# Adapter input products from each sample's own gathered columns, and a new order of VectorE's last additions

## What is computed

```python
def _lora_linear(x, W, A, B, adapter_indices):
    base = jnp.einsum('bsd,df->bsf', x, W)
    Ai = A[adapter_indices]
    Bi = B[adapter_indices]
    lora = jnp.einsum('bsr,brf->bsf', jnp.einsum('bsd,bdr->bsr', x, Ai), Bi)
    return base + lora
gate = _lora_linear(x, Wg, Ag, Bg, adapter_indices)
up = _lora_linear(x, Wu, Au, Bu, adapter_indices)
h = jax.nn.silu(gate) * up
return _lora_linear(h, Wd, Ad, Bd, adapter_indices)
```

## Time and profile before

| | |
|---|---|
| median of 3 runs | 1266.41 us (1262.3 to 1268.48) |
| the profiled execution | 1263.87 us, span 1261.8 us |
| PE busy | 1249.3 us, 99% of the span |
| DVE busy | 977.8 us, 77% |
| POOL busy | 665.7 us, 53% |
| ACT busy | 559.2 us, 44% |

### The profile page before, as it was taken

How to read it: one execution, slowest core, us unless ns; L and a number is a source line. 1 busy time by engine, 2 the same in 40 slices (tenths; PEclk the granted TensorE clock), 3 DMA queues, 4 the chain that set the end, 5 groups by cost and what they waited for, 6 DMA issues and landing times.

```text
span 1261.8 us, 17908 instructions
## 1 busy us (share of the span) xinstructions
PE 1249.3 (99%) x6204; PEld 1041.9 (83%) x6204; DVE 977.8 (77%) x1554; ACT 559.2 (44%) x993; POOL 665.7 (53%) x549
## 2 busy tenths in 40 slices
PE   8999999999999999999999999999999999999998
PEld 7788888888888888888888888888888888888886
DVE  6987777886788777788779768777888877777775
ACT  3744445444344444454444444444443434444432
POOL 4476555555635556545554556565555444445453
PEclk9999999999999999999999999999999999999999
DMA  5856345555965345445687444535477732243333
GB/s 193 299 177 221 121 119 166 159 146 170 378 203 189 105 122 150 128 131 175 218 316 218 158 126 147 153 120 136 146 289 267 229 93 89 70 117 101 118 92 109
DMA packets 141097, 210.11 MB, mean 167 GB/s; under 512 B 43473, under 2 KB 87761, under 8 KB 141009
## 3 DMA queue, kind: packets, MB, share of 16 engines
q1 hardware_dynamic: 118128, 137.03, 34.7%
q0 software_dynamic: 22016, 70.80, 17.0%
q10 hardware_dynamic: 864, 1.15, 0.2%
HBM read 164.89 MB, written 44.04 MB: 166 GB/s over the span
## 4 chain that ended last, share of the span: by engine, by line
PE 90%; DVE 5%; DMA 2%; issue 1%; ACT 1%; another core or an unknown queue 0%; SPq 0%; DVEq 0%; ACTq 0%
PE px L1544 28%; PE pd L1544 27%; PE py L1544 14%; PE pz L1544 7%; PE pz L1561 3%; PE pv L1590 2%; PE pv L1588 2%; PE pd L1822 2%; PE py L1561 2%; PE px L1561 1%; DVE wg_lo L1215 1%; DMA w_raw<-w_gu 1%; PE pd L1571 1%; PE pd L1665 0%; PE pd L1793 0%
## 5 line engine op out<-in xcount | busy, mean ns | idle before, releaser
L687 POOL TENSOR_TENSOR h_lo<-g,h_hi 128x512 fp32r<-128x512 f32 x127 | 184.3, 1451 | 336.2 <-ACT h_hi L809 335.5
L656 POOL DMA_INDIRECT b_got<-b_table,idx_b x192 | 197.5, 1029 | 58.5 <-issue 49.0
L1544 PE MATMUL px<-xo_hi,wg_hi 128*128 128x512 f32 x540 | 216.9, 402 | 2.1 <-ACT up L809 0.7
L1347 DVE TENSOR_TENSOR acc<-pd,acc 128x512 f32<-128x512 f32 x252 | 168.0, 686 | 63.0 <-PE pd L1544 59.9
L1215 DVE TENSOR_TENSOR wg_lo<-w_raw,wg_hi 128x512 fp32r<-128x512 f32 (+1 forms) x268 | 192.1, 720 | 31.1 <-issue 19.5
L1544 PE MATMUL px<-xo_hi,wg_lo 128*128 128x512 f32 x540 | 211.8, 392 | 0.0
L1544 PE MATMUL px<-xo_lo,wg_hi 128*128 128x512 f32 x540 | 210.4, 390 | 0.0
L809 ACT ACTIVATE wg_hi<-w_raw 128x512 fp32r<-128x512 f32 (+1 forms) x272 | 153.0, 570 | 114.9 <-PE py L1561 70.3
L1544 PE MATMUL pd<-wd_hi,h_hi 128*128 128x512 f32 x512 | 202.8, 396 | 0.0
L1544 PE MATMUL pd<-wd_lo,h_hi 128*128 128x512 f32 x512 | 201.0, 393 | 0.0
L1544 PE MATMUL pd<-wd_hi,h_lo 128*128 128x512 f32 x512 | 199.8, 390 | 0.0
(11 more groups left out here) (292 smaller groups left out, 2403.1 us busy)
## 6 DMA issues: line engine op xcount, KB each, us to landing
w_raw<-w_gu SPq DMA_DIRECT2D x68, 512.0 KB
wd_raw<-w_dn SPq DMA_DIRECT2D x64, 256.0 KB
xo_hi<-xops SPq DMA_DIRECT2D x21, 512.0 KB, 5.9
xo_lo<-xops SPq DMA_DIRECT2D x21, 512.0 KB, 6.9
acc<-x SPq DMA_DIRECT2D x8, 1024.0 KB, 8.4
ad_raw<-ad_table SPq DMA_DIRECT2D x16, 512.0 KB
xops<-st_hi SPq DMA_DIRECT2D x24, 256.0 KB, 2.7
xops<-st_lo SPq DMA_DIRECT2D x24, 256.0 KB, 2.9
```

The lines of the kernel that those rows point to most:

```text
L656: gp.indirect_dma_start(out=dst, out_offset=None, in_=rows_of, in_offset=bass.IndirectOffsetOnAxis(ap=rows.bitcast(U32), axis=0)).then_inc ...
L687: return gp.tensor_tensor(dst, src_raw, src_hi, ALU.subtract)
L1347: ins = dve.tensor_tensor(dst, pd[j][:, :], dst, ALU.add)
L1544: ins = pe.matmul(psum, w_parts[wi], x_parts[xi], start=(start and i == 0), stop=(stop and i == 2), skip_group_check=more)
```

## The change

**Own columns.** For quarters 1 to 3, 16 gathers (`gather_own`) fetch for each sample the A columns of its own adapter, gate and up, into `st_lo`: 128 rows of 512 bytes a gather. ACT and DVE split them into four groups of 128x512 in place of the adapters' weight groups; one extra subtraction (`own_difference`) makes the second half's weights. `own_products` replaces the 7 products: 24 matmuls of 256 columns for each half. There are now two results in place of four. `c11`, `u3`, `c12`, the `sums` of unit -1 and its weight load are gone, and two `ua_high` and two `ua_low` remain. `select` keeps its 12 matmuls, and for these quarters uses one fixed `sel_own`, so `selectors` is gone there. ACT makes `sel_own` once, with 12 small activations in block 14 of quarter 0, from 9 small DVE instructions in block 13.

**Moves.** POOL's 16 gathers stand in blocks 13 (5, after `h_low(q, 13, 1)`), 14 (2 before `h_low(q, 14, 1)`, 5 after it) and 15 (4, ahead of `h_low(q, 15, 0)`). The four `gather_ad` move from blocks 13 and 14 to behind block 15 and into unit -1, their stores on SP too. DVE's `v_low(q, 0)`, `own_difference` and two low parts stand between the additions of the last two down phases. SP loads A22 ahead of S2, and the weights of block 0 in block 14. Small index tiles share `f_one`.

**The end.** `finish(3, 0)` is cut up: pair 0, `v_mask(3, 1)`, pair 1, `v_low(3, 1)`, pairs 2 and 3.

The core of the diff:

```diff
+            def own_products(q, t):
+                for cp in range(2):
+                    k = ((A11, A12), (S1, A22))[t][cp]
+                    tokens_ready(q, k)
+                    pe.wait_ge(w_done[2 * t + cp], unit(q, -1) + 1)
+                    w_parts = own_homes(2 * t + cp)
+                    for c in range(2):
+                        for a in range(2):
...
+                            for i, (wi, xi) in enumerate(((0, 0), (0, 1), (1, 0))):
+                                ins = pe.matmul(ua_bank(q, t, 0)[:, a * HALF:(a + 1) * HALF], w_parts[wi][:, cols],
+                                                (xo_hi, xo_lo)[xi][:, k, tok], start=(cp == c == a == i == 0),
+                                                stop=True, skip_group_check=True)
+                ins.then_inc(own_mm, 1)
...
@@ PE, the units @@
-                adapters = b == -1
+                if b == -1:
+                    pe.wait_ge(c12_done, k)
+                    own_products(q, 0)
+                    pe.wait_ge(c21_kept, k)
+                    own_products(q, 1)
+                    pe.wait_ge(down_add, 5 * q * 2 * SUPER)
+                    finish(q - 1, 0)
+                    pe.wait_ge(c22_done, k)
+                    select(q, 0)
+                    continue
...
@@ POOL, the units @@
                 if b % 2:
-                    gp.wait_ge(c11_done, n)
+                    gp.wait_ge(c11_done, k)
                     ad_low(q, b // 2)
...
+                if to_own and b == BLOCKS - 1:
+                    gather_own(q + 1, range(12, 16))
                 gathers = b % 2 and (q, b) != (QUARTERS - 1, BLOCKS - 1)
                 if (q, b) != (0, 0):
                     h_low(q, b, 0)
...
-                if b == BLOCKS - 2 and q + 1 < QUARTERS:
-                    for g in range(2, AD_GROUPS):
-                        gather_ad(q + 1, g)
+                if to_own and b == BLOCKS - 2:
+                    gather_own(q + 1, range(5, 7))
...
                 if b == BLOCKS - 3 and q + 1 < QUARTERS:
-                    for g in range(2):
-                        gather_ad(q + 1, g)
+                    gather_own(q + 1, range(0, 5))
+                if to_own and b == BLOCKS - 2:
+                    gather_own(q + 1, range(7, 12))
+                if to_own and b == BLOCKS - 1:
+                    for g in range(4):
+                        gp.wait_ge(w_done[g], n + 2)
+                    for g in range(2):
+                        gather_ad(q + 1, g)
...
@@ ACT, the units @@
+                if b == -1:
                     v_lower(q - 1, 0)
                     v_high(q - 1, 0)
+                    weights_high(n, 3)
                     v_lower(q - 1, 1)
+                    ua_high(q, 0)
+                    weights_high(n + 1, 0)
+                    weights_high(n + 1, 1)
+                    weights_high(n + 1, 3)
+                    ua_high(q, 1)
+                    v_high(q - 1, 1)
+                    weights_high(n + 1, 2)
+                    continue
...
+                if (q, b) == (0, BLOCKS - 2):
+                    act.wait_ge(sel_mm, 2)
+                    act.wait_ge(slots_done, 1)
+                    for m in range(2):
+                        for s in range(HS + 2):
...
+                            ins = act.activation(sel_own[:, m, :, lo:hi], pattern_kept[:, :, 0:hi - lo], ACT.Copy,
+                                                 scale=slot_mask[:, at:at + 1])
+                    ins.then_inc(sel_done, 1)
...
@@ DVE, the units @@
                 if b == -1:
-                    v_low(q - 1, 0)
-                    c11(n)
-                    u3(n)
-                    ua_low(q, 0, 0)
-                    c12(n)
-                    ua_low(q, 1, 1)
-                    ua_low(q, 0, 1)
                     sums(n + 1)
+                    ua_low(q, 0)
                     weights_low(n + 1, 0)
-                    ua_low(q, 1, 0)
+                    weights_low(n + 1, 1)
+                    finish(q - 1, 0, (0,))
+                    ua_low(q, 1)
+                    finish(q - 1, 0, (1,))
                     select(q, 0)
-                    weights_low(n + 1, 1)
+                    finish(q - 1, 0, (2, 3))
                     weights_low(n + 1, 2)
-                    finish(q - 1, 0)
                     weights_low(n + 1, 3)
-                    selectors(q, 1)
                     continue
...
-                c11(n)
+                c11(k)
+                if to_own:
+                    weights_low(n + 1, 0)
...
                     if last and phase_at[2]:
-                        finish(q, 0)
+                        finish(q, 0, (0,))
+                        v_mask(q, 1)
+                        finish(q, 0, (1,))
                     if last:
                         v_low(q, phase_at[2])
+                    if last and phase_at[2]:
+                        finish(q, 0, (2, 3))
+                    if to_own and not phase_at[2]:
+                        v_low(q, 0)
+                        own_difference(q + 1)
+                        weights_low(n + 1, 2)
+                        weights_low(n + 1, 3)
```

More of the change, by code:

```diff
@@ L315, in cond_resid_kernel @@
         down_add = sem("down_add")
+        own_got = [sem(f"own_got{t}") for t in range(2)]
+        own_diff = sem("own_diff")
+        own_mm = sem("own_mm")
+        slots_done = sem("slots_done")
         ua_hi_done = sem("ua_hi_done")
@@ L741, in _ @@
                         gather_bd(q - 1, 1)
+                        for g in range(2, AD_GROUPS):
+                            gather_ad(q, g)
                     continue
@@ L941, in _ @@
                     ad_high(q, b // 2)
+                k = blocks_done(q, b)
+                to_own = b == BLOCKS - 1 and not last
                 if b == -1:
@@ L1041, in _ @@
                     keep_c21()
-                act.wait_ge(p3_mm, n)
-                if not last and b > 1:
+                act.wait_ge(p3_mm, k)
+                if not last and not to_own and b > 1:
                     weights_high(n + 1, 2)
@@ L1059, in _ @@
                     weights_high(n + 1, 2)
-                if not last:
+                if not last and not to_own:
                     weights_high(n + 1, 3)
@@ L1348, in add_down @@
                     ins.then_inc(down_add, 1)
-                if m == SUPER - 1:
+                if m == SUPER - 1 and not ends:
                     v_mask(q, t)
@@ L1370, in finish, with own_difference, ua_low @@
                     dve.tensor_tensor(dst, finish_bank(q, t, j)[:, :], dst, ALU.add).then_inc(y_add, 1)
-            def ua_low(q, t, m):
-                src = ((g0, up0), (g1, up1))[t][m] if q else first_banks[t][m]
-                dve.wait_ge(ua_hi_done, 4 * q + ua_order(q, t, m))
-                dve.tensor_tensor(h_lo[:, t, m, :], src[:, :], h_hi[:, t, m, :], ALU.subtract).then_inc(ua_done, 1)
+            def own_difference(q):
+                dve.wait_ge(own_got[1], q * 2 * TP * 16)
+                first, last_two = (own(cp)[:, 2 * TP:QS, :, :] for cp in range(2))
+                dve.tensor_tensor(last_two, last_two, first, ALU.subtract).then_inc(own_diff, 1)
+            def ua_low(q, t, m=0):
+                dve.wait_ge(ua_hi_done, ua_made(q, t, m))
+                dve.tensor_tensor(h_lo[:, t, m, :], ua_bank(q, t, m)[:, :], h_hi[:, t, m, :], ALU.subtract).then_inc(ua_done, 1)
             def c11(n):
@@ L1492, in _ @@
                     half_numbers()
-                if not last and not late:
+                if (q, b) == (0, BLOCKS - 3):
+                    dve.wait_ge(layer_mm, QP)
+                    dve.tensor_copy(pattern_kept, pattern)
+                    for at in range(2 * HS):
+                        ins = dve.tensor_scalar(slot_mask[:, at:at + 1], p_f[:, 0:1], float(at), None, ALU.is_equal)
+                    ins.then_inc(slots_done, 1)
+                if not last and not late and not to_own:
                     sums(n + 1)
@@ L1515, in _ @@
                     token_low(q, parts_at(q, b))
-                c12(n)
+                c12(k)
                 gate0()
```

328 lines of the change are left out of this document (179 added, 149 removed).

## The result

The changed kernel took 1268.48 us in the median of 20 runs (1266.11 to 1270.74), the kernel before beside it 1263.70 (1261.26 to 1268.48): ratio 1.0034, 95% interval 1.0027 to 1.0041. I had predicted 1261.6 with a range up to 1266.5, a gain of 4.8 us; it is a loss of 4.8. (The forecast stood on a median of 3 runs, 1266.41, which is 2.7 above the kernel before as measured here; on that base a gain of 4.8 would have been 1258.9.) No measurable difference at 0.5%, but the sign and the range are wrong. The experiments measured the same program four times more: 1.0043 on one chip, and 1.0003, 0.9999 and 0.9997 on two others. So there are two things to explain: why nothing is gained where I expected 4.8, and why the result and one of the chips lose 4 to 6 more.

The account below looks back on a forecast made before the run. PE, busy for 99% of the span, was taken as the bound. The sum -11.9 + 6.6 + 0.3 + 1.0 + 0.1 - 0.9 = -4.8 us gave a predicted median of 1261.6 us, range 1254.5 to 1266.5.

Parts of the forecast that it names:

- The mechanism of the gain: PE's products in unit -1: 9.61 us replaced by 5.64, saving 3.97 a unit, 11.9 in all.
- the products do not shrink: Rival on PE's own products: 256 columns cost more, for example 0.17 us each; +2.8, 1269.2 us; chance 0.04.
- That delay is not added to the other: Quarter boundary: A22's wait and h_low(15, 0)'s lateness share the same clock time, so only one is charged.
- the block of DVE by POOL: Block 15: POOL's subtractions hold DVE's low parts ahead of u3, so A22 waits up to 2.4 us.
- the lateness of `h_low(15, 0)`: Block 15: behind four gathers it ends at 333.3, PE needs it at 331.09; PE waits 2.2 us.
- the 6.6 of the sum: PE's wait of 2.2 us for POOL's h_low(15, 0) at three boundaries, with ends 0 and 9.0.
- The gathers' price: POOL's 16 gathers in blocks 13 to 15: 1.275 us each, making h_low(15, 0) end at 333.3.
- DVE at the boundary: After the last down phase (end T): ua_low(1) ends at T + 8.5, needed at T + 8.8; 0.3 us in all.
- shared reading adds up: Rival at the boundary: A22's wait also delays h(15, 0), 3.7 us a boundary; -0.3, 1266.1 us; chance 0.12.
- The selectors: Block 14 of quarter 0: ACT's twelve activations delay u3, so A22 waits 1.0 us once (ends 0 and 1.3).
- The end: Kernel end: PE's 0.96 us wait for v_low goes; gain 0.9 us (ends 0 and 1.0).
- Gathers landing late: Rival at the boundary: the last gathers land past 11 us, each boundary loses 3.7 us more; 1273 us; chance 0.06.

Follow-up runs that it names:

- e1: Changed kernel with DVE's two low parts of the own columns behind gate0 of block 15 instead of ahead of u3: 1259.07 us, 0.9974 of the kernel before.
- f3: e1 measured again, beside f0_after on the same chip: 1259.23 us, 0.9979 of the kernel before.
- e8: Changed kernel with POOL's gathers 9 to 11 moved behind the two down_low and ahead of ad_low, DVE's order kept: 1259.30 us, 0.9968 of the kernel before.
- g2: e8 with ACT's twelve selector activations split into two sixes: 1259.89 us, 0.9979 of the kernel before.
- after_again: The changed kernel measured again without an edit: 1263.11 us, 1.0003 of the kernel before.
- f0_after: The changed kernel without an edit, as control of other runs on the same chip: 1262.31 us, 0.9999 of the kernel before.
- e5: The kernel before with only the change's new order of DVE's last additions at the end: 1261.86 us, 0.9992 of the kernel before.
- e6: e1 with POOL's queue in block 15 reordered, two gathers ahead of each h_low: 1265.02 us, 1.0009 of the kernel before.
- e9: e6 with ACT's selectors in two sixes and POOL's four bd gathers issued ahead of three b_got gathers: 1274.07 us, 1.0087 of the kernel before.

## Why the prediction was wrong

**The mechanism of the gain held.** 48 matmuls at 0.1175 were to take 5.64 us; they took 5.78. Saved per unit: 3.83 for 3.97, in all 11.5 for 11.9. The rival "the products do not shrink" is out.

**The wait had the size I gave; its place was the other one of the two.** "That delay is not added to the other" held. I had both delays, priced the block of DVE by POOL at up to 2.4 and the lateness of `h_low(15, 0)` at 2.2, and said that PE pays for one of them only. I put the price on POOL's; the one that PE meets first is `u3`. It costs 2.0 to 2.1 us, 6.3 in all for the 6.6 of the sum, and masks the second, which is an idle time of 1.46 in e1 and costs 1.7 there. The gathers' price held too: in PE's time `h_low(15, 0)` ended at 332.7 (336.59 less 3.92), for 333.3.

**The first step that failed: the sum has no clock in it.** The granted clock was 1.00 wherever I read it, and I charged each wait in the middle of dense matmuls with its length alone. Yet 11 of the 27 waits for `u3` of 1.75 to 1.94 us in the traces are followed by a stretch at 0.50, and each such stretch cost 1.7 us. The changed kernel's mean clock on P and R is 0.9980 to 0.9982, the kernel before's 0.9995 to 0.9998: 0.0016 of 1262 us is 2.0, the largest single item of the error there. In the result's own runs the mean was 0.9973. The kernels that got rid of those waits (e1, f3, e8, g2) have 0.9994 to 0.9996.

**The second step that failed: "DVE at the boundary", "ua_low(1) ends at T + 8.5".** I charged 0.3 for it, with ends 0 and 3. On P it held: T + 8.15 in after_again. In the result's execution it was T + 11.0, since ACT could take t = 0 only at T + 7.25. PE stood 2.4 us ahead of the three blocks 0 in place of my 0.3, and 1.6 more ahead of `finish`, where the sum has nothing. These 4.0 us are most of what turns nothing into the loss of 4.8; on Q, with 5.8, it is the same. I had let the signal of t = 0 come when its matmuls are done, and nothing in the rows of before that I read says otherwise. Why it comes late stays open. It does so in the stretch in which PE dispatches a matmul every 0.12 us, new through this change, while the DMA engines are full (share 1.03). Both hold on P and R as well, where nothing stalls, so together they are not enough; that either has a part in it was argued, not shown.

**Of shared SBUF the trace's reading was right.** The Trainium skill ("SBUF — State Buffer", who interferes with whom), as I read it, would have let DVE in behind each single POOL instruction. The earlier trace rows had shown a subtraction held through two; here a low part was held through all that were left of the three (327.44 to 330.05), and e8 shows it unhindered. It was so at every boundary of the nine traces with this order: the low part ended 0.5 to 0.6 us behind the last of POOL's, whether it had begun in the first of them or in the second. None shows DVE get in between consecutive POOL subtractions. On P and R the rival "shared reading adds up" came nearest (a gain of 0.3), and in the result's runs "the products do not shrink" (a loss of 2.8), both by luck: `h_low(15, 0)` cost nothing on top of `u3`, and the products did shrink.

**The small terms.** The selectors cost 0.9 for 1.0. The end gave 0.84 for 0.9. DVE at the boundary cost nothing on P. Not in the sum were waits for bd, 0.3 to 1.1 an execution, and 0.2 to 0.5 more than before for ACT (up), together some 1 us. The sum with these sizes: -11.5 + 6.3 + 0.9 - 0.8 + 1.0 + 2.0 = -2.1, where the ratios say +0.4, -0.1 and -0.4 on P and R, each with an uncertainty of 1.1 to 1.5. So some 2 us are not accounted for. Matmul by matmul, from 60 us on, after_again gains 2.9 us on the trace of before and f0_after 1.5, about what the sum has for one clock drop and for two. What is missing would then lie ahead of that, where single executions differ by as much: the five traces of the changed kernel stand there from 0.4 us ahead of before's to 1.6 behind it, and e5's 1.4 ahead. Whether the change costs something there isn't shown.

**Gathers landing late** did not occur for the own columns; it did for bd once the other waits were gone (e6), by POOL's queue and the full engines together. My range ended at 1266.5, since I had let the terms left at zero add nothing: clock, bd and late signals can only add, and they did.

## What to carry to other kernels

When work is added ahead of a queue's subtractions, look not only at who waits for them, but at what stands on the other engine at the time to which they move: here a push of 4.6 us put them on top of two-input subtractions of DVE, and keeping them apart (e8) was worth as much as moving the victim (e1). Where two delays fall into the same stretch of time, charge the one that PE meets first, and know that the second comes up when the first is removed; then the third. A wait of 1.8 to 1.9 us between dense matmuls cost nearly twice its length (1.9 + 1.7) in 11 cases of 27 here, since the clock can fall behind it: give such a wait that price with a chance. And measure such a kernel beside its control on the same chip.

## What the runs showed of the hardware

- A DVE subtraction with both inputs in SBUF stood through three consecutive POOL subtractions (3.2 to 3.3 us for 0.7 of work; 2.6 where it began in the second of them) and ended 0.5 to 0.6 us behind the last of them, at every boundary of nine traces. With POOL's subtractions elsewhere it took its usual time (e8).
- Behind 11 of 27 waits of PE of 1.75 to 1.94 us, in an execution behind none to two of its three, came a stretch at 0.50 of the clock, which cost 1.7 us each time. Behind 13 waits of 1.45 to 1.53 it never came, nor behind the two of 1.81 (e8, g2) and the one of 2.27 (the result's execution); what decides it is not shown. On P a mean clock of 0.9979 to 0.9988 goes with the first kind, 0.9995 to 0.9996 with the second.
- 256 columns behind a full weight load cost 0.120 us in a stream of 48, for 0.1175 in a group of four.
- In such a stream, with the DMA engines full, ACT could take the result of t = 0 only at T + 6.7 to 7.3 in the result's execution and at T + 6.7 to 8.3 on Q (10.7 and more in e9), where PE's dispatch also stood still for 0.8 to 1.1 us at a time. On P and R it came at T + 3.1, with the DMA engines as full. The same program therefore differs by 0.4 to 0.5% between these series, while the kernel before agrees within some 0.1% (medians 1262.4 to 1263.7): an experiment on such a kernel needs its control on the same chip. The cause stays open.
